# The expert stage of a conv, attention and mixture-of-experts kernel: 56 tiles in a loop of eight, or all written out

## What is computed

```python
x = relu(x + softplus(residual_scale) * bn(conv1x1(relu(bn(conv3x3(relu(bn(conv1x1(x)))))))))   # 256 -> 64 -> 64 -> 256
t = tokens(x)                                   # 16 x 196 = 3136 tokens of 256
t = t + linear_attention(ln(t))                 # 16 heads of 16
flat = ln(t)
probs = softmax(flat @ gate_w + gate_b)         # 8 experts, the top 2 with their shares normalised
for e in range(8):
    h = gelu(flat @ w1[e] + b1[e])              # 256 -> 1024
    out = out + comb[:, e:e + 1] * (h @ w2[e] + b2[e])   # 1024 -> 256
t = t + out
```

## Time and profile before

| | us |
|---|---|
| median of 3 runs | 736.99 (736.5 to 738.81) |
| profiled execution | 728.51 |
| its span | 726.8 |
| expert stage in it, from the first row load to the end | 313.7 to 726.8 |
| PE busy | 610.5 (84%) |
| DVE busy | 461.4 (63%) |
| ACT busy | 317.6 (44%) |
| POOL busy | 212.0 (29%) |

### The profile page before, as it was taken

One profiled execution on the slowest core, in us unless ns is written; L12 is line 12 of the kernel. 1 busy time (PEld: TensorE's weight loads), 2 busy tenths in 40 slices (PEclk: granted clock), 3 DMA queues, 4 the chain that ended last, 5 costly groups with the idle time before them and its releaser, 6 DMA issues.

```text
span 726.8 us, 14377 instructions
## 1 busy us (share of the span) xinstructions
PE 610.5 (84%) x3882; PEld 539.8 (74%) x3883; DVE 461.4 (63%) x1492; ACT 317.6 (44%) x626; POOL 212.0 (29%) x193
## 2 busy tenths in 40 slices
PE   6662589989889976149999999999999999999982
PEld 3641477777768965137998998998898899899872
DVE  2788799989898885515555555565564565555550
ACT  1645577867676542013433433333343334334330
POOL 5320121212755665711222122122122121221221
PEclk9876699999999995569999999999999999999996
DMA  9490888878877962421256372734626528322211
GB/s 278 131 345 2 323 313 298 302 258 296 292 282 259 372 236 75 135 55 30 40 161 189 84 251 45 269 77 127 208 44 177 169 38 293 54 37 44 30 16 15
DMA packets 50488, 120.83 MB, mean 166 GB/s; under 512 B 7564, under 2 KB 39184, under 8 KB 44304
## 3 DMA queue, kind: packets, MB, share of 16 engines
q1 hardware_dynamic: 30128, 98.07, 37.2%
q0 software_dynamic: 11136, 14.00, 11.5%
q10 hardware_dynamic: 9184, 8.28, 4.2%
HBM read 68.22 MB, written 52.11 MB: 166 GB/s over the span
## 4 chain that ended last, share of the span: by engine, by line
PE 58%; DVE 22%; issue 6%; ACT 5%; POOL 2%; DMA 2%; DVEq 2%; SPq 2%; ACTq 0%; POOLq 0%
PE ps L846 42%; PE ps L873 6%; DVE wset L1115 4%; PE ps L684 2%; DVE stt L1026 2%; POOL rows_by_expert L440 2%; PE ps L839 2%; PE ps L778 1%; PE ps L741 1%; ACT xh L540 1%; DVE tc L1017 1%; DMA wset<-in_ew 1%; DVE img L1109 1%; DVE bst L996 1%; PE ps L730 1%
## 5 line engine op out<-in xcount | busy, mean ns | idle before, releaser
L462 POOL DMA_INDIRECT out<-ys,xr x56 | 86.7, 1548 | 318.7 <-DVE ys L1382 248.4
L846 PE MATMUL ps<-wset,hTh 128*128 x896 | 163.6, 283 | 6.9 <-DVE hTl L1350 6.9
L846 PEld LDWEIGHTS ps<-wset,hTh 128*128 128x128 f32 x896 | 141.8, 190 | 14.9 <-issue 10.8
L846 PE MATMUL ps<-wset,xrTh 128*128 x448 | 147.4, 410 | 0.0
L635 ACT ACTIVATE hb<-hb 128x512 f32<-128x512 f32 x112 | 70.5, 632 | 140.1 <-DVE hb L1371 140.1
L846 PE MATMUL ps<-wset,hTl 128*128 x448 | 126.3, 282 | 0.0
L641 ACT CAST hTh<-ps 128x512 fp32r<-128x512 f32 x112 | 60.2, 590 | 102.4 <-PE ps L873 102.0
L1377 DVE TENSOR_TENSOR yb<-ps,bset 128x256 f32<-128x256 f32 x56 | 23.8, 424 | 124.6 <-PE ps L846 124.6
L846 PEld LDWEIGHTS ps<-wset,xrTh 128*128 128x128 f32 x448 | 81.1, 191 | 15.6
L846 PE MATMUL ps<-wset,xrTl 128*128 x224 | 89.5, 400 | 0.0
L1371 DVE TENSOR_TENSOR hb<-ps,bset 128x512 f32<-128x512 f32 x112 | 75.9, 685 | 16.8 <-PE ps L846 16.6
(11 more groups left out here) (181 smaller groups left out, 943.2 us busy)
## 6 DMA issues: line engine op xcount, KB each, us to landing
split_weights<-wset SPq DMA_DIRECT2D x16, 2048.0 KB, 7.4
wset<-split_weights SPq DMA_DIRECT2D x32, 1024.0 KB, 7.1
wset<-in_ew SPq DMA_DIRECT2D x16, 1024.0 KB, 10.1
xr<-rows_by_expert ACTq DMA_DIRECT2D x56, 132.5 KB, 2.2
bset<-in_eb SPq DMA_DIRECT2D x8, 640.0 KB, 9.1
img<-in_x SPq DMA_DIRECT2D x8, 392.0 KB, 6.4
out<-img SPq DMA_DIRECT2D x16, 196.0 KB
rows_by_expert<-rows,slot POOLq DMA_INDIRECT x64, 3.1
```

What stands on the lines that cost most here:

```text
L462: pool.indirect_dma_start(out, bass.IndirectOffsetOnAxis(xr[:, r % XR, C + E:ROW].bitcast(U32), 0), ys[:, r % YS, :], None, compute_op=ALU ...
L846: last = pe.matmul(dst, rows_k[:, k * 128:(k + 1) * 128], wset[:, bass.ds(column(k) + rest, width)], start=(k == 0 and n == 0), stop=(k == ...
```

## The change

On all four engines the loop is gone, and the 56 tiles are written out one after the other. Tile numbers, semaphore values and the index of the table reads are constants. `experts_of` is called once ahead of each four tiles, for g = 1 to 13. What a slot does and the order of its steps are the same, and the numbers of the experts still come from the table.

```diff
@@ POOL
-            for i in range(4):
-                add_rows(i, i)
-            with pool.Fori(0, SLOTS // 8 - 1) as g:
-                for r in range(8):
-                    add_rows(8 * g + 4 + r, r + 4)
-            for i in range(SLOTS - 4, SLOTS):
+            for i in range(SLOTS):
                 add_rows(i, i)
@@ ACT
-            for m in range(4):
-                act_slot(m, m)
-            with act.Fori(0, SLOTS // 8 - 1) as g:
-                for r in range(8):
-                    act_slot(8 * g + 4 + r, r + 4)
-            for m in range(SLOTS - 4, SLOTS + 2):
-                act_slot(m, m % 8)
+            for m in range(SLOTS + 2):
+                act_slot(m, m % XR)
@@ PE
             for m in range(4):
                 pe_slot(m, m % XR)
-            with pe.Fori(0, SLOTS // 8 - 1) as g:
-
-                of = experts_of(2 * g + 1), experts_of(2 * g + 2)
-                for q in range(8):
-                    mine = of[q // 4]
-                    pe_slot(8 * g + 4 + q, (q + 4) % XR, mine[q % 4], mine[q % 4 + 1], g * 16 + (q // 4) * 16 + 16)
-            of = experts_of(SLOTS // 4 - 1)
-            for q in range(4):
-                pe_slot(SLOTS - 4 + q, (SLOTS - 4 + q) % XR, of[q], of[q + 1])
+            for g in range(1, SLOTS // 4):
+                of = experts_of(g)
+                for q in range(4):
+                    pe_slot(4 * g + q, (4 * g + q) % XR, of[q], of[q + 1])
@@ DVE
-            with dve.Fori(0, SLOTS // 8 - 1) as g:
-
-                of = experts_of(2 * g + 1), experts_of(2 * g + 2)
-                for q in range(8):
-                    mine = of[q // 4]
-                    vec_slot(8 * g + 4 + q, (q + 4) % XR, mine[q % 4], mine[q % 4 + 1], mine[q % 4 + 2],
-                             g * 16 + (q // 4) * 16 + 16)
-            of = experts_of(SLOTS // 4 - 1)
-            for q in range(4):
-                vec_slot(SLOTS - 4 + q, (SLOTS - 4 + q) % XR, of[q], of[q + 1], of[q + 2])
+            for g in range(1, SLOTS // 4):
+                of = experts_of(g)
+                for q in range(4):
+                    vec_slot(4 * g + q, (4 * g + q) % XR, of[q], of[q + 1], of[q + 2])
```

## The result

| | before | after |
|---|---|---|
| median | 735.76 us (732.85 to 738.81, 6 runs) | 723.84 us (722.94 to 730.2, 6 runs) |
| profiled execution / span | 728.51 / 726.8 us | 723.74 / 722.0 us |

The ratio of the runs is 0.9873, with a 95% interval of 0.9845 to 0.9902: 9.3 us less of 735.76, between 7.2 and 11.4. I had forecast 4.7. Two more timings of the pair, each on one chip, have 0.9909 (0.9881 to 0.9937; 6.7 us of 734.95) and 0.9877 (0.9858 to 0.9895; 9.0 us of 730.07).

The account below looks back on a forecast made before the run. PE was taken to bound ordinary slots (6.734 us), leaving only losses around table reads: 8.47 us before, 3.77 after, 4.70 saved. From a median of 736.99 that gives 732.3 us, range 728.5 to 736.0.

Parts of the forecast that it names:

- The losses of before, 8.47 us: Time lost around table reads: five back edges 7.14, tile 52 0.29, tile 4 0.28, PE's wait at the entry 0.76 us.
- the 0.76 us at the loop's entry: PE's idle time on issue ahead of tile 4, from two reads and the loop's register set-up; taken as gone.
- tile 4 shows 0.28: Slot of tile 4, first in the loop, lasts 7.01 us, 0.28 too long; held as evidence against R2.
- R2: Rival, chance 0.06: tile 52's 0.29 comes from leaving the loop, not its read; all 8.47 go, 728.5 us.
- Six reads move: Each iteration's second read moves to the head of tiles 8, 16, 24, 32, 40, 48; 1.74 us added.
- thirteen heads cost 0.29 each: Starts of four tiles (4, 8, ... 52) each lose tile 52's 0.29 us; 3.77 us of losses after the change.
- my bounds for the six moved reads: Six moved reads cost 3.96 us in all if uncovered, nil if fully covered; 0.29 each was taken.
- Register arithmetic ... I cost it at nothing: Register arithmetic for tile numbers goes on PE, DVE, ACT and POOL; no gain counted, as PE's work and waits hide it.
- PE's lateness and DVE's gap: At a back edge PE reaches its first transpose 0.22 us late; DVE idles 1.78 us ahead of `hTl`; 1.43 lost each.
- R1: Rival, chance 0.08: branch costs nothing, each read costs DVE 0.89 us anywhere; 13 heads at 0.52, 1.7 us saved, 735.3.
- R3: Rival, chance 0.06: PE's instruction fetches meet expert weight loads, about six of 20 holding PE 1.1 us; 738.9 us, slower.
- The forecast of their number (20): Five further iterations written out need about 20 more instruction packets on either queue, q8 and q14, with no time lost.

Follow-up runs that it names:

- the one with more code: The changed kernel with 20 more waits per slot on DVE, for a semaphore that is long there; stage 404.1 us, against 400.8 to 401.8 of the changed kernel.

## Why the prediction was wrong

*What bounds the kernel: right.* Ordinary slots stayed at 6.71 to 6.75 us, PE's own work, in all fourteen profiles. Waits for constants in place of register values made none of them shorter.

*The losses of before, 8.47 us: right as a sum.* The back edges' excess vanished (14.88 to 13.50), and the 0.76 us at the loop's entry went too (slot 3 lasts 7.88 in place of 8.79 us, and slot 4 begins with no issue wait). One reading in it was off without changing the sum: the row of tile 4 ends 0.16 us behind the start of the next slot's transposes. From start to start the slot lasts 6.85 us, and the 0.16 belongs to the entry. So "tile 4 shows 0.28", which I held against R2, should have been 0.12.

*Six reads move, and thirteen heads cost 0.29 each: this step failed.* "The slot of tile 52 ... begins with a single table read, exactly as tiles 4, 8, 12 ... will": the read was the same, but not what stood ahead of it. DVE's row step of slot 51 was still in the loop body, with its register arithmetic (0.21 us idle ahead of L1391), and behind it came the loop's end. Those made the gap 0.66 and not 0.49, and `hTl` 0.3 us late. The heads cost 0.03 or nothing, except two with an instruction fetch (0.29 each) and tile 52 (0.13); 3.77 us became about 0.6. The loop with one read for four tiles shows the same from the other side, 0.22 us for a mid-body read; there the register arithmetic alone makes `hTl` 0.24 us late, so most of the 0.3 is its, and the little that is left goes with the loop's end. The 0.29 of tile 52 before is itself two things: the first product of the second layer comes 0.18 us late, and the second follows it after 0.22 us in place of 0.12. PE loses those 0.10 at each late start, at tiles 12 and 24 of after as well. Tile 52 of after has them without a late start, in all three profiles, and no run shows why. Of my bounds for the six moved reads it is the lower one that came true, and R2, to which I gave 0.06, named the mechanism.

*"Register arithmetic ... I cost it at nothing": wrong in one place.* It is free wherever PE hides it, in every ordinary slot. It is not free in the short stretch between DVE's wait for PE (L1377) and `hTl`, when a read shares that stretch.

*PE's lateness and DVE's gap:* I counted both into one excess, rightly. The runs with one engine show that they overlap: the excess of 1.41 stays with PE alone written out, is 0.34 with DVE alone, and 0.03 with both.

*The drain, slots 56 and 57:* I left it out as unchanged, and its code is. Slot 56 became 0.35 us shorter all the same, since DVE is 0.4 us less late there. Before and after, ahead of `hTl`:

```profile
700.86 1.29 DVE L1350 TENSOR_TENSOR hTl<-ps,hTh 128x512 fp32r<-128x512 f32 x2 [1.51 <-issue]
697.65 1.29 DVE L1335 TENSOR_TENSOR hTl<-ps,hTh 128x512 fp32r<-128x512 f32 x2 [1.10 <-issue]
```

Before, a q14 packet lies at 701.4 us, beside this instruction; after, there is none near it. In the five profiles with DVE in the loop and separate reads in slot 56 the gap is 1.51 to 1.53 with such a packet, and in the six with DVE written out and separate reads 1.10 to 1.11 without one. It is DVE's instruction fetch again, and where it falls is luck.

And PE's clock in the last 24 products differs from run to run. The windows of these products before:

```profile
708.43:713.06 4.63, 4.63 (x24) 4.42 (x24) 0.00 (x0) 0.00 (x0) 0.53 (x1) 0.63 0.29 32
```

and after:

```profile
705.30:708.42 3.12, 3.11 (x24) 2.91 (x24) 0.00 (x0) 0.00 (x0) 0.53 (x1) 1.00 0.39 42
```

That is 1.5 us. The granted clock, 1.00 (2.4 GHz) until then, falls to 0.50 (1.2 GHz) from 708.98 to 712.39 us and is back at 1.00 behind it. It is seen in both profiles of before, in one of the three of after (0.67 over 4.30 us) and in the one with more code, and in none of the other ten. Ahead of it PE stands idle 2.07 us in either of the two shown. Whether the change bears on it stays open.

*The sum now:* 7.9 us in the slots to 55 (8.47 less 0.6), 0.35 in slot 56, and on average about 1 us of clock in the drain: 9.3, against 9.5 between the mean stages (410.7 and 401.3) and 9.3 by the ratio.

*The range.* Its lower end, 728.5, let all of the 8.47 us go from a median of 736.99. Six runs put that median at 735.76, and 9.3 less is 726.5 us, below the range already: 1.2 us by the starting point and 0.8 by what the sum had left out, slot 56 and the clock. The rest down to 723.84, that is up to the 11.9 us between the medians, is scatter of the timed runs (722.9 to 730.2 after, 732.9 to 738.8 before), which I had let into the upper end of the range and not into the lower.

*R1 and R3:* no head has a gap of 0.89, and the 20 q8 packets between 394 and 670 us show no wait of PE beside them. The forecast of their number (20) was right for q8; q14 has 12 there, where I had put 20 too. The Trainium skill (Advanced Engine Details and Errata, Control Flow Timing) has about 108 ns for the branch. With the reads moved away, the gap at the back edge measures 0.35 us on DVE, with the loop's counter and registers in it, and it is covered. No run here measures the branch alone.

## What to carry to other kernels

The back edge of this loop was not dear for its branch. Look at what the sequencer must do between the last wait and the instruction on which the bottleneck engine waits. Spreading two table reads and putting them behind that instruction gave in this stage all that writing out 56 tiles gave, with half the instruction packets on q8 (400.9 us, in one profile). And when a saving is read off one slot that already has the new form, check that what stands ahead of it will be the same too.

## What the runs showed of the hardware

- The untouched first part, the same in all kernels, varied from 316.0 to 327.5 us over fourteen profiles, partly by the chip (317.0 to 318.1 on two, 321.6 to 327.5 on two others), while the expert stage repeated to 0.1 to 1 us. One profile's difference in span (4.8 us) would have confirmed a forecast (4.7 us) that was wrong by half.
